# Seven background transfers of the attention stage issued ahead of its loop instead of behind it

## The reference, cut to what matters

```python
x = x + tanh(g_xattn[0]) * L0_xattn(layernorm(x), ctx, ctx)       # attention, 8 heads
x = x + tanh(g_ffn[0])   * L0_ffn(layernorm(x), ...)              # 8 experts, top 2
x = x + tanh(g_xattn[1]) * L1_xattn(layernorm(x), ctx, ...)       # scan, summary, layernorm
x = x + tanh(g_ffn[1])   * L1_ffn(layernorm(x), ...)              # 64 experts, top 4, and shared experts
```

```python
logits = xf @ w_gate; top_logits, top_idx = top_k(logits, 2); weights = softmax(top_logits)
h0, h1 = sorted_x @ wi_0[e], sorted_x @ wi_1[e]
out = (silu(h0) * h1) @ wo[e]
```

## Time and profile before

| | before |
|---|---|
| median of 3 runs | 1118.6 us (1116.68 to 1118.72) |
| the profiled execution's own time | 1116.68 us |
| its span, first to last instruction | 1115.0 us |
| mean granted TensorE clock | 0.972 |
| busy: PE, DVE, POOL, ACT | 92%, 65%, 53%, 45% |
| SyncE's queue (q1): data, share of 16 DMA engines | 160.66 MB, 43.2% |

### The profile page before, as it was taken

The page is one execution under the profiler, slowest core; times in us unless marked ns, Lnnn a source line. Parts: engine busy times, 40 slices in busy tenths (PEclk is TensorE's granted clock), DMA queues, the critical chain, the costliest instruction groups (busy, mean ns, idle before and its releaser), DMA issues. The chain is left out here.

```text
span 1115.0 us, 18847 instructions
## 1 busy us (share of the span) xinstructions
PE 1026.0 (92%) x5364; PEld 739.1 (66%) x5364; DVE 724.2 (65%) x1703; ACT 501.1 (45%) x880; POOL 590.1 (53%) x556
## 2 busy tenths in 40 slices
PE   5999999999869999998899999999999999999960
PEld 3556555565327777775399478577778888888850
DVE  4578777776358888885689248267406676666650
ACT  3666656655238888886432201311303333333320
POOL 7566676674426667665524646356332344434551
PEclk9999999999989999999899999999999999999985
DMA  8567555578744333331540241043269999999629
GB/s 257 162 219 248 195 162 187 197 248 281 260 141 162 106 111 104 103 112 68 186 141 21 87 138 46 11 136 114 85 210 335 337 325 309 291 314 342 187 28 194
DMA packets 128254, 199.49 MB, mean 179 GB/s; under 512 B 35975, under 2 KB 44167, under 8 KB 128186
## 3 DMA queue, kind: packets, MB, share of 16 engines
q1 hardware_dynamic: 106538, 160.66, 43.2%
q0 software_dynamic: 21360, 37.48, 13.2%
q10 hardware_dynamic: 288, 0.52, 0.1%
HBM read 133.10 MB, written 87.56 MB: 198 GB/s over the span
## 5 line engine op out<-in xcount | busy, mean ns | idle before, releaser
L935 POOL TENSOR_TENSOR m_down_lo<-wo,m_down_hi 128x512 fp32r<-128x512 f32 x78 | 129.5, 1680 | 76.1 <-ACT m_down_hi L1030 76.1
L543 PE MATMUL bank<-win,vT 128*128 128x512 f32 x256 | 123.5, 596 | 0.0
L703 DVE TENSOR_REDUCE negmax<-bank 128x1 bf16<-128x512 f32 x128 | 85.6, 672 | 37.9 <-PE bank L550 37.5
L633 ACT ACTIVATE win<-bank 128x512 f32<-128x512 f32 x128 | 69.5, 594 | 89.7 <-PE bank L535 86.9
L1044 DVE TENSOR_TENSOR m_up_lo<-w,m_up_hi 128x1024 fp32r<-128x1024 f32 x78 | 97.9, 1256 | 13.2 <-ACT m_up_hi L1002 11.7
L2035 POOL DMA_INDIRECT out<-m_y,m_token x32 | 51.4, 1605 | 88.7 <-DMA out<-m_y,m_token 36.7
L1264 POOL DMA_INDIRECT tab<-stage_up,slot x64 | 65.5, 1023 | 53.7 <-DVE slot L1610 35.7
L2065 PE MATMUL bank<-y,m_w 128*128 128x128 f32 x736 | 89.7, 275 | 0.0
L2035 POOL DMA_INDIRECT sums<-m_y,m_token x32 | 52.3, 1633 | 69.4 <-DVE m_y L2129 35.6
L2179 ACT ACTIVATE sh_gate_a<-bank 128x512 f32<-128x512 f32 (+1 forms) x40 | 20.5, 513 | 150.8 <-PE bank L2172 121.2
L2065 PEld LDWEIGHTS bank<-y,m_w 128*128 128x128 f32 x736 | 86.4, 193 | 0.1
(11 more groups left out here) (297 smaller groups left out, 2502.6 us busy)
## 6 DMA issues: line engine op xcount, KB each, us to landing
tab<-zeros SPq DMA_DIRECT2D x16, 1056.0 KB
m_w<-in_L_ffn_Wg SPq DMA_DIRECT2D x46, 256.0 KB
m_w<-in_L_ffn_Wu SPq DMA_DIRECT2D x46, 256.0 KB
m_w<-in_L_ffn_Wd SPq DMA_DIRECT2D x46, 256.0 KB
m_x<-tab SPq DMA_DIRECT2D x39, 256.0 KB, 2.7
ytab<-m_y SPq DMA_DIRECT2D x39, 256.0 KB, 2.1
stage_up<-tab SPq DMA_DIRECT2D x32, 264.0 KB
m_x<-tab SPq DMA_DIRECT2D x32, 264.0 KB
```

Source lines behind the costliest of these rows:

```text
L543: nc.tensor.matmul(pO[s * 2 + h][:], vT[:, s, sb_, h:h + 2, :].rearrange("p a c -> p (a c)"), probs[:, sb_ % 2, h, :], start=(sb_ == 0), s ...
L633: nc.scalar.activation(probs[:, b % 2, h, :], pS[h][:], ACT.Exp, scale=1.0 / HEAD).then_inc(p_ready, 1)
L703: nc.vector.tensor_reduce(negmax[:, s, m:m + 1], rough_bank(k, m)[:], AX.X, ALU.max, negate=True).then_inc(pm_read, 1)
L935: nc.gpsimd.tensor_tensor(dn_lo[:, m, :], row(wo0, e * MB + m), dn_hi[:, m, :], ALU.subtract).then_inc(dn_lo_ready, 1)
```

## The change

The zeros for the last rows of `tab0`, and `behind(0)`, are issued ahead of the loop, behind the values of tiles 0 and 1, instead of behind the loop.

```diff
@@ -313,6 +313,8 @@
             for t in range(2):
                 load_v(sp, t, t)
             sp.wait_ge(consts_ready, 1)
+            sp.dma_start(T["tab0"][DUMMY_ROW:, :].rearrange("(r p) d -> p r d", p=P),
+                         zeros[:, 0:D].unsqueeze(1).broadcast_to([P, E0, D])).then_inc(s_zero1, 16)
             t1 = T["tab1"].rearrange("(n r p) d -> n p r d", p=P, n=ZERO_CHUNKS)
...
+            behind(0)
             with sp.Fori(1, TILES // 2) as u:
...
                     load_v(sp, t, n)
-            behind(0)
-            sp.dma_start(T["tab0"][DUMMY_ROW:, :].rearrange("(r p) d -> p r d", p=P),
-                         zeros[:, 0:D].unsqueeze(1).broadcast_to([P, E0, D])).then_inc(s_zero1, 16)
```

## The result

| | before | after |
|---|---|---|
| median of 5 runs | 1117.29 us (1114.08 to 1118.72) | 1126.36 us (1122.29 to 1128.64) |
| ratio, 95% interval | | 1.0077 [1.0047, 1.0105] |
| the profiled execution's own time | 1116.68 us | 1120.38 us |
| its span | 1115.0 us | 1118.6 us |
| mean granted TensorE clock | 0.972 | 0.966 |

The change makes the kernel about 9 us slower; I had forecast 1124 us with a range to 1129. The profiled execution of after is faster than all five timed runs (1120.38 against 1122.29 us and more), so single positions in its trace say more than its span.

The account below looks back on a forecast made before the run. TensorE was taken as the bound in steady attention, a GpSimd chain at its end. Start loss 6.5 plus clock 2.3 minus end gain 3.1 made +5.7 us on 1118.6, given as 1124 us; range 1118.5 to 1129.

Parts of the forecast that it names:

- The backlog at the start: Tile 2's keys queue behind the moved transfers, landing at 42.6 us; TensorE loses 6.5 us (ends 3.2 and 9.7).
- The clock behind it: After TensorE's wait for tile 2's keys, half clock for 4.6 us loses 2.3 us (ends 0 and 2.3).
- Completion in the order of issue: SyncE's queue is served in issue order, so tile 2's keys wait; early completion would make the 6.5 us loss vanish.
- Rival 1: At L659 of tile 2: keys not held up, nothing lost, the end gives 3.1 us; 1115.5 us, chance 0.10.
- rival 3: The backlog also reaches tile 3's keys, which miss by some 2 us; +9.7 us, 1128.3 us, chance 0.12.
- The end: End of attention: seven transfers gone from the queue, next stage 3.1 us earlier relative to the loop (ends 0 and 5.4).
- tile 13's add and TensorE behind it: At attention's end, the add's 2.68 us wait and TensorE's 1.67 us behind it go; -1.7 us to all following.
- tile 14: ScalarE's L639: With an earlier add, ScalarE's copy follows TensorE's last values directly at 285.3 instead of 288.28; -3.0 us in all.
- tile 15: its add: Stays 7.04 us behind its scatter, covered by context transfers; at 295.0 instead of 298.05, -3.1 us.
- tile 15: `xn` (L665): ScalarE's last normalization follows tile 15's add in an unchanged chain, so it also gains 3.1 us.
- what follows is one chain and keeps its length: Behind tile 15's add, statistics through last scatters keep their length, so the next stage gains the full 3.1 us.
- rival 4: The end gives nothing: the drain's excess has another cause or context transfers replace it; +8.8 us, 1127.4 us, chance 0.05.

Follow-up runs that it names:

- the busy wait: After plus 28 TensorE matmuls with unread results, ahead of the wait for tile 2's keys in step 1; ratio to before 1.0084.
- the version with the gaps: Against after, behind(0) moved behind the keys of tile 3 and tab0's zeros behind those of tile 5, inside the loop; ratio to before 0.9987.
- the new order: Fewer TensorE context products ahead of the last transposes, more behind; ratio to before 1.0054 as an edit of after, 1.0025 as an edit of before.
- the gaps with the new order: Seven transfers in gaps behind the keys of tiles 3 and 5, plus TensorE's context products in later places; ratios to before 0.9974 and 0.9959.
- the first four experiments: Zeros alone ahead (1.0001 of before), behind(0) alone ahead (1.0041), the transfers in gaps (0.9987), after with later context products (1.0054).

## Why the prediction was right, and where it was wrong

**The backlog at the start: right.** Forecast: keys usable at 42.6 us; measured 43.38 and 43.22. Forecast of the stall: 6.5 us; TensorE's first rough product is 7.36 us late (44.62 - 37.26). The runs with one part ahead show that bytes in front of the keys set this, and that slack is used up first: the 2.10 MB of zeros alone cost no wait at L659, and a late L659 makes TensorE late by 2.1 us less (4.31 and 2.18 us with `behind(0)`, 9.49 and 7.36 in after; forecast 2.2).

**The clock behind it: right in the trace.** Forecast 2.3; step 2's scores are 9.43 us late (51.19 - 41.76), 2.1 more than the first product. The Trainium skill, "TensorE: Matmul & The Clock Gate", section "HAM oscillation", has a wait for data send the array back to its half clock; the run with the busy wait agrees, since the clock stayed at 1.00 there and fell to 0.50 in the other kernels in which TensorE waited for the keys. Start together: 9.3 to 9.4, forecast 8.8.

**Completion in the order of issue: as forecast, to within 1 us.** The last keys of tile 2 landed behind what was issued ahead of them: with the zeros alone, the zeros landed at 28.1 us (18.05 + 10.0) and the keys issued at 22.6 at 28.9 (6.3 later); with `behind(0)` alone, its last zeros at 36.1 (23.22 + 12.9) and the last keys at 38.2 (28.9 + 9.3); in after the keys were there at 43.4. The Trainium skill, "DMA: Bandwidth & Descriptors", section "Queues, rings and completion order", leaves room for completion out of order. The run with `behind(0)` alone shows a little of it: the first two of the four key transfers landed at 35.3 and 35.9 us (25.1 + 10.2 and 26.0 + 9.9), ahead of the zeros issued before them. It doesn't help, since L659 starts only when all four are there. Rival 1 did not occur. Nor did rival 3: tile 3's keys had no wait.

**The end: the step that failed.** The prediction had -3.1; the trace has +1.7 (10.98 - 9.3), and by the timed difference it is -0.2 (9.1 - 9.3). Either way the gain of 3.1 us is missing. Its links one by one, each as delay against before:

| link | forecast, against the start's loss | measured delay | against 9.3 |
|---|---|---|---|
| tile 13's add and TensorE behind it | -1.7 | last scores +7.87 (290.44 - 282.57) | -1.4 |
| tile 14: ScalarE's L639 | -3.0 | +6.60 (294.88 - 288.28) | -2.7 |
| tile 15: its add | -3.1 | +6.22 (304.27 - 298.05) | -3.1 |
| tile 15: `xn` (L665) | -3.1 | +6.23 (308.06 - 301.83) | -3.1 |
| context landed, L496 | not in the forecast | +7.94 (303.89 - 295.95) | -1.4 |
| last transposes, L603 | -3.1 | +10.96 (313.74 - 302.78) | +1.7 |

The last column is against the loss right behind the start. Of this, 0.7 us had come back before the end began: step for step the transposes are 9.3 to 9.5 us late up to 113 us, and 8.6 us from 130 us on (247.97 against 239.32), because before has a wait there that after has not: its add (L450) at 112.06 waits 1.53 us, and TensorE 0.84 us behind it, at 115.53 (in after the add waits 0.78 and TensorE not at all). So the -1.4 at the last scores are 0.7 of the loop and 0.7 of tile 13's wait (0.94 instead of 1.67 us, where the forecast had it gone), and their nearness to -1.7 is partly luck; counted from the end of the loop, the chain gained 2.4 us and the last transposes lost 2.3.

The chain through GpSimd gained most or all of what was forecast. What failed is the sentence that what follows is one chain and keeps its length. Between `xn` and L603 stand TensorE's products of the late context. The context is issued when the last scores are done and lands a fixed time behind them: 13.4 us in before (295.95 - 282.57), 13.5 in after. It could gain only the 1.4 us that the last scores gained. TensorE came to it earlier and so waited 3.53 instead of 1.99 us, and behind this longer wait its clock fell to half. From the landing to the end of the six further products it took 9.85 us (313.74 - 303.89) instead of 5.58 (298.79 + 2.74 - 295.95): 4.3 us. Without those 4.3 us L603 would have been late by 6.7 us, an end of -2.6. So the gain earned in front of it turned into a wait, and the wait into a cold clock.

That the order is what turns it is shown by the runs with fewer products in front: with it, `xn` decides again, and some 3 us come back in after and 1.5 to 3.1 in the version with the gaps (0.9987 against 0.9974 and 0.9959). That 4.3 us are the clock's is read from the durations and not shown by a run in which only that clock is changed, but two traces come near it: with the zeros alone and with `behind(0)` alone the same ten products stood behind waits of 3.44 and 3.61 us, the clock was back at 1.00 from 301 and from 307 us, and from the landing to L603 it took 6.9 and 7.2 us. In after, its repeat, the gaps and the busy wait (waits of 3.53 to 4.17 us) it stayed at half until L603 or about 1 us before, and it took 9.6 to 10.0.

**The sum.** Forecast +5.7, measured +9.1 (ratio 1.0077), in the range because the range had been drawn to hold rivals 3 and 4. In size the outcome is nearest to rival 4 (+8.8), but not by its mechanism: the drain did give its gain. So the range held by luck where the end is concerned.

**What stays open.** The traces' offsets at L990 exceed the timed differences by 0.2 to 4.4 us (with the zeros alone 1.7 against 0.1, `behind(0)` alone 7.9 against 4.5, the gaps 2.7 against -1.4, the new order 8.7 against 6.0, the gaps with the new order -2.7 against -2.9 and -0.1 against -4.6, each to the first profile of before). Part of it is that a profiled execution can be slower than the median of its runs: by 2.0 us with `behind(0)` alone, 1.7 with the gaps, 0.3 with the new order, 1.7 in the second profile of the gaps with the new order. The rest I have not found.

## What to carry to other kernels

Ahead of an awaited transfer, count bytes: what lies in front costs nothing up to the reserve and the full rate beyond it, so background work belongs behind the urgent transfer and in front of a long pause, not ahead of it and not in the last rush. Before you book a gain on a chain, look at what else its end has to join, in the engine's own program order: here a product that waited for a transfer with a fixed start stood in between. And a gain that makes TensorE arrive early at such a transfer can come out as a loss, since a longer wait can also cost the clock.

## What the runs showed of the hardware

- **A short wait can also lower the clock.** With `behind(0)` alone ahead, one wait of 1.67 us was followed by a granted clock of 0.50 from 41 to 43 us, while the same 1.67 us of the earlier trace rows left it at 1.00. With the new order in before, six context products took 4.43 us without a wait recorded at them, behind a stretch in which TensorE was idle in pieces. Behind tile 13's add, waits of 1.67 and 1.91 us (before, busy wait) left it at 1.00, and waits of 1.89 and 1.94 us (the new order in after and in before) were followed by about 3 us at half. I had expected this only behind waits of some 5 us. So the length of the wait alone does not tell the cases apart; what does was not tested.
- **A scatter's landing depends on the other queue.** The same scatter of 128 rows took 6.7 to 6.9 us with SyncE's queue full and 2.7 to 2.8 with a DMA share of 0.26; GpSimd's add behind the drain waited 3.71 and 0.32 us. It was even faster than in the steady part (4.4).
- **A 2 KB transfer takes the queue's time.** L361 landed 13.5 us after its issue in before and 6.5 in after, behind L360's megabyte.
- **Profiles differ by group, whatever the kernel.** The stretch from L990 to the end took 796.6 and 797.4 us in two profiles of before and 798.9 in the repeat of after, but 789.2 in the first profile of after and 788.6 to 789.8 in the first four experiments. The profiles of one group of runs, on one chip, lie within 1.2 to 3.0 us. A difference between two single profiles of that size is no evidence unless both ran on one chip.
